# Attention scores of four head pairs in one PE step, steps put off while no bank is idle, and the inverse denominators turned by a transpose

## What is computed

```
h = layer_norm(x); q, k, v = split(h @ w_qkv.T)              # 16 heads of 16 numbers
for each window c of 128 queries and each head:
    scores = q[c] @ concat(k[c-1], k[c]).T * scale             # 128 x 256, masked to a band
    attn = softmax(scores); out[c] = attn @ concat(v[c-1], v[c])
x = x + out @ w_o.T, then norm, a GELU MLP, residual
```

## Time and profile before

| | |
|---|---|
| median of 3 runs | 3789.12 us (3778.06 to 3798.62) |
| profiled execution, its own time | 3792.8 us |
| its span in the trace | 3790.9 us |
| PE busy | 3120.8 us, 82% |
| POOL busy | 2860.8 us, 75% |
| DVE busy | 2831.7 us, 75% |
| ACT busy | 2403.9 us, 63% |
| granted TensorE clock, mean | 0.91 of full speed |

### The profile page before, as it was taken

One profiled execution on the slowest core, in us unless ns is written; L12 is line 12 of the kernel. 1 busy time (PEld: TensorE's weight loads), 2 busy tenths in 40 slices (PEclk: granted clock), 3 DMA queues, 4 the chain that ended last, 5 costly groups with the idle time before them and its releaser, 6 DMA issues.

```text
span 3790.9 us, 58550 instructions
## 1 busy us (share of the span) xinstructions
PE 3120.8 (82%) x17648; PEld 1915.7 (51%) x17648; DVE 2831.7 (75%) x6080; ACT 2403.9 (63%) x5299; POOL 2860.8 (75%) x2511
## 2 busy tenths in 40 slices
PE   5878788887988989798898979889797988977457
PEld 3545354453645546465464636555464654644235
DVE  3357878787787878878787877778788787879860
ACT  5567667575767757676675857667576766754331
POOL 1118889887888879887897978888798878977770
PEclk9998888898999999899898989989998998988678
DMA  2026777777777778776877867787787768789980
GB/s 70 6 78 182 195 193 201 202 206 211 190 209 224 190 216 210 229 196 182 232 212 208 219 200 207 194 225 188 220 213 227 203 185 232 210 241 242 254 224 34
DMA packets 422204, 735.60 MB, mean 194 GB/s; under 512 B 53306, under 2 KB 99010, under 8 KB 421890
## 3 DMA queue, kind: packets, MB, share of 16 engines
q1 hardware_dynamic: 421890, 731.85, 70.7%
HBM read 647.80 MB, written 83.89 MB: 193 GB/s over the span
## 4 chain that ended last, share of the span: by engine, by line
PE 52%; DVE 16%; POOL 10%; ACT 9%; issue 8%; DMA 3%; SPq 1%; DVEq 0%; ACTq 0%; POOLq 0%
PE bank L454 13%; PE bank L462 8%; PE bank L577 6%; PE bank L720 5%; POOL u_rows L1455 5%; PE bank L487 5%; DVE u_rows L1266 4%; POOL u_rows L1448 4%; PE bank L499 4%; PE bank L656 4%; PE bank L708 3%; DMA u_rows<-u_dram 3%; PE bank L515 2%; ACT prob L775 2%; DVE region_b L1198 1%
## 5 line engine op out<-in xcount | busy, mean ns | idle before, releaser
L1455 POOL TENSOR_TENSOR u_rows<-u_rows,c_rows 128x512 f32<-128x512 f32 x1024 | 1339.1, 1311 | 261.9 <-DVE state L1271 208.3
L1448 POOL TENSOR_TENSOR u_rows<-u_rows,b_rows 128x512 f32<-128x512 f32 x960 | 1275.0, 1329 | 33.0 <-DMA u_rows<-u_dram 32.7
L938 ACT ACTIVATE bank<-d_rows,a_rep 128x512 f32<-128x512 f32 x1024 | 697.7, 689 | 283.7 <-DMA d_rows<-delta_dram 127.1
L1266 DVE TENSOR_TENSOR_SCAN u_rows<-bank,state,u_rows 128x512 f32<-128x512 f32 x512 | 642.6, 1270 | 67.6 <-ACT bank L938 64.6
L1266 DVE TENSOR_TENSOR_SCAN u_rows<-bank,u_rows 128x512 f32<-128x512 f32 x512 | 622.7, 1216 | 62.9 <-ACT bank L938 60.4
L656 PE MATMUL bank<-u_rows,sum_n 128*32 128x512 f32 x2048 | 307.1, 674 | 310.3 <-POOL u_rows L1455 303.6
L775 ACT ACTIVATE prob<-prob,neg_max 128x256 f32<-128x256 f32 x1024 | 511.6, 507 | 40.7 <-DVE neg_max L1050 40.4
L1050 DVE CUSTOM_DVE_ANT_0 prob<-bank,band 128x256 f32<-128x256 f32 x896 | 336.9, 416 | 145.5 <-PE bank L487 117.0
L499 PE MATMUL bank<-ident,prob 128*128 128x128 f32 x2048 | 332.4, 290 | 107.2 <-ACT prob L775 66.7
L499 PEld LDWEIGHTS bank<-ident,prob 128*128 128x128 f32 x2048 | 243.1, 147 | 265.0 <-issue 192.1
L487 PE MATMUL bank<-kT,q_own 32*128 32x256 f32 x2048 | 304.3, 417 | 46.4 <-DVE neg_max L1050 26.6
(11 more groups left out here) (163 smaller groups left out, 5661.6 us busy)
## 6 DMA issues: line engine op xcount, KB each, us to landing
u_rows<-u_dram SPq DMA_DIRECT2D x1024, 256.0 KB, 5.5
d_rows<-delta_dram SPq DMA_DIRECT2D x1024, 256.0 KB, 5.3
w<-in_W SPq DMA_DIRECT2D x28, 1024.0 KB
zs_dram<-region_b SPq DMA_DIRECT2D x64, 256.0 KB, 2.2
xc_dram<-region_b SPq DMA_DIRECT2D x64, 256.0 KB, 2.5
delta_dram<-region_b SPq DMA_DIRECT2D x64, 256.0 KB, 2.8
u_dram<-region_b SPq DMA_DIRECT2D x64, 256.0 KB, 2.1
yg<-xc_dram SPq DMA_DIRECT2D x64, 256.0 KB, 5.0
```

The lines of the kernel that those rows point to most:

```text
L938: e.activation(banks[at.bank][:, :], delta_of(i, k), ACT.Exp, scale=a_rep[:, j:j + 1]).then_inc(filled[at.bank], 1)
L1266: e.tensor_tensor_scan(rows, banks[at.bank][:, :], rows, state[:, k:k + 1] if i % 2 else 0.0, ALU.mult, ALU.add).then_inc(drained[at.bank], 1)
L1448: e.tensor_tensor(rows, rows, b_rows[:, :], ALU.mult).then_inc(bx_ready.sem, 1)
L1455: e.tensor_tensor(rows, rows, c_rows[:, :], ALU.mult).then_inc(hc_ready.sem, 1)
```

## The change

1. `scores_of(u)` now does the pairs 4u to 4u+3 at beats 0, 8, 16, ...: four `free` waits at once, then eight matmuls, four for the even heads and four for the odd ones. Four row groups and four banks follow one another.
2. The masks of the four pairs stand at beats 1, 2, 3 and 6 of the eight (before: 1, 2, 5 and 6).
3. `schedule` and `banks_of` become one function that lays out the list and the banks together. At each place it takes the earliest step for which as many banks are idle as it begins uses (and whose thread before it is done); a step for which they aren't is put off.
4. The turn of `rden_wide` is `e.transpose` in the place of `e.matmul` with the identity as the moving operand.

```diff
+MASK_AT = (1, 2, 3, 6)
...
-            out += [(f"s{n}", at, at + 1 + odd), (f"p{n}", at + 5 + odd, at + 6 + 2 * odd)]
+            out += [(f"s{n}", ATT0 + 8 * (n // 4), ATT0 + 8 * (n // 4) + MASK_AT[n % 4]), (f"p{n}", at + 5 + odd, at + 6 + 2 * odd)]
...
+    def earlier(thread, i):
+
+        out = [] if THREADS[thread][0] == ("scan",) else [(thread, i - 1)]
+        if thread:
+            out.append((thread - 1, i | 1 if THREADS[thread][0] == ("fetch",) else i))
+        return out
+
+    order, uses = [], {}
+    idle, counted, signalled = list(range(8)), [0] * 8, [0] * 8
+    while chains:
+        for key, chain in sorted(chains.items(), key=lambda c: c[1][0][:2]):
+            _, _, stage, i, step = chain[0]
+            shared = stage == "scan" and shared_inputs(i, batches)
+            names = begins.get((stage, shared, step), ())
+            if len(names) <= len(idle) and not any(c in chains for c in earlier(*key)):
+                break
+        else:
+            raise AssertionError("no bank is idle")
+        order.append((stage, i, step))
+        for name in names:
             bank = idle.pop(0)
             uses[stage, i, name] = Use(bank, counted[bank], signalled[bank])
...
-            def scores_of(v):
-
-                if v == 0:
+            def scores_of(u):
+
+                if u == 0:
                     for name in ("q0", "q1", "k0", "k1"):
                         e.wait_ge(*gone(use(name)))
-                for n in (2 * v, 2 * v + 1):
+                for n in range(4 * u, 4 * u + 4):
                     e.wait_ge(*free(use(f"s{n}")))
                 for par in range(2):
-                    for n in (2 * v, 2 * v + 1):
+                    for n in range(4 * u, 4 * u + 4):
...
-                e.matmul(banks[at.bank][:, P:2 * P], rden_wide[:, k * P:(k + 1) * P], ident[:, :],
-                         start=True, stop=True).then_inc(filled[at.bank], 1)
+                e.transpose(banks[at.bank][:, P:2 * P], rden_wide[:, k * P:(k + 1) * P],
+                            ident[:, :]).then_inc(filled[at.bank], 1)
...
-                if beat % 4 == 0 and beat < 64:
-                    scores_of(beat // 4)
+                if beat % 8 == 0 and beat < 64:
+                    scores_of(beat // 8)
...
-                v, at = divmod(beat, 4)
-                if at in (1, 2) and v < 16:
-                    masked(2 * v + at - 1)
+                u, at = divmod(beat, 8)
+                if at in MASK_AT and u < 8:
+                    masked(4 * u + MASK_AT.index(at))
```

More of the change, by code:

```diff
@@ L111, in uses_of, with __init__ @@
     return []
+class Use:
+    def __init__(self, bank, n, f):
+        self.bank, self.n, self.f = bank, n, f
 def schedule(batches):
-    at = []
+    chains = {}
     for thread, (stages, lag, begin, end) in enumerate(THREADS):
@@ L119, in schedule @@
         for i in range(2 * batches):
-            spent = 0.0
+            chain, spent = [], 0.0
             for stage in stages:
[L122 to L127, removed]
+                if stage == "route" and i % 2 == 0:
+                    continue
+                which = i // 2 if stage == "route" else i
                 for step, cost in enumerate(COSTS[stage]):
-                    at.append((i + lag + begin + (end - begin) * spent / total, thread, stage, which, step))
+                    chain.append((i + lag + begin + (end - begin) * spent / total, thread, stage, which, step))
                     spent += cost
-    return [(stage, which, step) for _, _, stage, which, step in sorted(at, key=lambda s: s[:2])]
-class Use:
-    def __init__(self, bank, n, f):
-        self.bank, self.n, self.f = bank, n, f
-def banks_of(order, batches):
+            if chain:
+                chains[thread, i] = chain
     begins, ends = {}, {}
@@ L159, in banks_of @@
             idle.append(uses[stage, i, name].bank)
-    return uses
+        del chain[0]
+        if not chain:
+            del chains[key]
+    return order, uses
 def build_block_stack(nc, d):
@@ L185, in build_block_stack @@
     assert WINDOW == P and SEQ % G == 0 and HD == 16 and GROUPS == 2 and ED // EL == TILES and KE * 16 == TILES
-    order = schedule(BATCH)
-    uses = banks_of(order, BATCH)
+    order, uses = schedule(BATCH)
     with ExitStack() as ctx:
```

## The result

| | before | after |
|---|---|---|
| median, 20 runs each | 3791.35 us | 3809.35 us (3800.82 to 3827.49) |
| ratio | | 1.0052, 95% interval 1.0039 to 1.0064 |
| profiled execution, its own time | 3792.8 us | 3806.71 us |
| PE busy | 3120.8 us | 2983.7 us |
| span less PE busy | 670.1 us | 821.2 us |

The forecast was 3759 us and faster; the kernel is slower by 18 us between the medians. The range (3690 to 3865) holds the time, the sign was missed. PE has 137 us less busy time and 151 us more idle time. These two are the whole result, since the span is PE's busy time plus the rest: -137.1 + 151.1 = +14 us in the two profiled executions. By the ratio of the runs the change costs 20 us (0.0052 x 3791).

What follows compares the result with a forecast made beforehand. No engine was taken to bound the whole; PE was busiest, with 52% of the chain. Terms -93 - 11 + 65 + 5 = -34 us from 3792.8 gave 3759 us, range 3690 to 3865 (forecast's own 3725 to 3795, chance 0.32).

Steps and rivals of the forecast that it cites:

- The PE terms: PE's scores with four row groups at once, -93 us, and the turn of rden_wide as a transpose, -11 us.
- The turn's own 11: PE's turn of rden_wide: one record instead of two saves 20 us of PE time, by PE's 52% -11 us.
- Bank hand-overs: PE's refills one step behind a drain: 187 added, 62 waits of 2.0 us, +65 us; bounds 0 and +161.
- ACT's +5: ACT's 65 added refills one step behind a drain delay decays: 22 waits of 1.3 us, by DVE's 16% +5 us.
- The rule read from the earlier trace: Steady period: a shorter PE step can move the end where PE, or PE and POOL, are full, not where DVE is.
- the slow rival: PE's queue in the attention beats: all 187 added bank waits at 1.66 us each, 3855 us; chance 0.26.
- Every close hand-over waits: PE's attention beats: each refill one step behind its drain waits 1.66 us, 310 us idle, 3855 us; chance 0.26.
- Its other sign: PE's granted clock falls below 0.91, beside idle behind drains growing by over 200 us, if every hand-over waits.
- POOL takes the gain: PE's sums wait for POOL, full from 1896 on, so most of the gain goes: -13 us, 3780 us; chance 0.17.
- Don't run together: Scores on PE: the four row groups serialize in pairs, so the first term is 0: 3852 us; chance 0.08.
- Free: Bank hand-overs cost nothing because they fall into PE's idle behind POOL: -104, 3689 us; chance 0.17.
- sign of being wrong: The scores' call on PE over 1.3 us, or PE's added idle outside 60 to 200 us.

Runs made afterwards that it cites:

- e10: The kernel before with each scores matmul issued twice into the same place; 3957.44 us, ratio 1.0451 to the kernel before.
- e9: The change with each scores matmul issued twice; 3863.66 us, ratio 1.0199 to the kernel before.
- e12: The kernel before, transposed-weights uses taking the bank freed last, so refills one step behind their drain go from 48 to 268; 3892.15 us, ratio 1.0274.
- e4: The change with a planner preferring steps whose banks have been idle for two steps or more, moving 962 steps; 3895.98 us, ratio 1.0278 to the kernel before.
- e13: The change with the scan's decays written one beat later (DECAY_AT -1 instead of -2); 3767.18 us, ratio 0.9928 to the kernel before.
- e14: The kernel before with the scan's decays one beat later, as control for e13; 3796.65 us, ratio 1.0024 to the kernel before.
- e18: e13 with weights uses taking the bank freed last, list and work the same; 3895.27 us, ratio 1.0292 to the kernel before.
- e16: The change with four pairs at once for only two of a group's eight fours, and decays one beat later; 3791.32 us, ratio 1.0006 to the kernel before.
- e2: The change with the eight matmuls of a scores call issued two row groups at a time; 3805.86 us, ratio 1.0046 to the kernel before.
- e1: The kernel before with only the turn of rden_wide made a transpose; 3787.74 us, ratio 0.9994 to the kernel before.

## Why the prediction was wrong

**The PE terms held in PE's time; their worth is uncertain.** -93 and -11 were the forecast for 153 us of PE time, -104 together. Busy time fell by 137; the scores' call is 1.15 us in the timeline against 1.13 for a call of half as many before, and the group went to 150.7 (forecast "about 155"). `rden_wide` has one record. The two groups alone fell by 175 us (153.6 and 21.2); the rest of PE's work, unchanged, was busy for longer. At e10's 75% the 137 are worth 103 us, at e9's 54% 74. The forecast's rate was 68% (104 of 153): 70% for the scores, from the 190 us that they had of the chain against 271 us of their calls, and 52% for the turn. That lies between the two. The turn's own 11 was not seen.

**The failed step is "Bank hand-overs".** It took one close refill in three as a wait of 2.0 us, 125 us of idle, and by the chain's 52% +65, with ACT's +5: 70 us. In its place stand 94 to 123 us (the 74 to 103 that PE's time was worth and the measured +20), and by e12's price 88 to 118, inside the bound of 161 that the step had kept. Of the 54 us between -34 and +20, 24 to 53 are this term's and the other 30 to 1 the worth of PE's time; the runs don't settle the split.

The idle time itself came out as forecast, and that was luck. PE's waits on a bank grew by 128 us where 125 stood, but as 118 more waits of 1.1 us, not 62 of 2.0. The rate was taken from one kind of hand-over, the turn behind a convolution. The kind that grew most, scores behind a scan (58.4 us in 53 times), was 4.4 us in 5 times before, and only 28 of the change's close refills are of this kind. A call that wants four banks at once waits for the last of them, close or not: e4 has no close refill at the scores and waits there for 112 us.

What was too small is what the idle costs. 52% of the 128 us is 67; the runs of equal work cost 0.57 to 1 us for each, so 73 to 128. PE's share of the chain says how much of PE's work lies on the path. At a late drain the path runs through the drain instead, as in the chain at 1943 to 1947, and the share of the idle engine says nothing about it; that is read from one place and argued for the others. And e12 showed a cost beside the idle that the step had no term for: PE busy for 32 us longer with the same work.

**The rule read from the earlier trace rows was right and was not used.** "In the first two a shorter PE step can move the end": it can, and by the same reasoning so can a wait put there. DVE at 11.79 of 12 us was named as what makes drains late, but only for the slow rival.

**The rivals.** "Every close hand-over waits" had the right place and direction: PE's queue in the attention beats, drains by DVE and ACT. It put the threshold at 200 us of idle at 52%; PE's waits behind DVE grew from 113 to 215 us and behind ACT from 220 to 284, 165 in all and 128 of them on banks, and that was already enough. Its other sign, a granted clock below 0.91, came with 0.906, but tells little: the kernel before had 0.911 in its profile and 0.908 on average in the runs beside the experiments. "POOL takes the gain" fell: L673's wait behind POOL shrank by 15 where 50 more were asked. "Don't run together" fell, the call is 1.15 us. "Free" fell.

The figure of the Trainium skill ("TensorE: Matmul & The Clock Gate", Part 3, Measured speedup vs the span model: 3.07 for four row tiles) would have made a call 1.33 us, by an estimate from that page's figure, which is for 512 columns. The trace has 1.15 for calls of 256 columns at the full clock, so the measurement stands against it here. The warning cited beside the slow rival (the Trainium skill, "TensorEngine Tiling (Array Packing)", Gotcha 1: PSUM Pressure) points at what decided: a close refill cost 0.29 us by e13 (47 us, and the 9 that e14's later decays cost, over 196), 0.47 by e12 and 0.62 by e18.

**The test of the prediction was too loose.** It asked for 60 to 200 us of new PE idle behind drains, and 128 came, 151 with the other waits. The call of 1.15 us passed as well. Neither sign of being wrong showed, and the forecast was wrong. For all PE time that is saved off the path turns into idle as well (153 less 104 is 49), so a forecast of -34 us already meant about 119 us of idle. A test on span less busy would have had to say 119, and 151 is then plainly too much.

**What stays open.** How much saved PE time is worth: 54% to 75% is from time added, and e16 got 7 us for 39. What a close refill of ACT costs. Why the list of e4 costs 50 us with no more waits on banks. Whether the lower clock alone keeps PE busy for longer where it waits more. A kernel with a fourth `prob` slot was not tried, so theory S is not settled.

## What to carry to other kernels

A step that does more at once also asks for more buffers at once. Count for each buffer how many steps lie between its drain and its refill before and after, and price the added close ones by a run: force close hand-overs in the old kernel with everything else the same. The count is a first guide only; e4 had 28 of them and waited as long as e12 with 268. Where they cost more than the work saved, look for a neighbour that holds a buffer too early; here moving the scan's decays one beat later turned +0.5% into -0.7%. And do not price idle time behind a late drain by the waiting engine's share of the chain: that was 52%, and the runs cost 0.57 to 1.

## What the hardware showed beyond that

**Four row groups run together in full.** Doubling the work of a call tells its slope free of the start. All of these are durations of the timeline at the full clock, where all but a few calls of a run have the same length; a call of the kernel before has 1.13 us (the chain's 1.06 leaves out what overlaps the next). With two row groups (e10 against before) it went from 1.13 us to

```profile
1937.03 2.10 PE L488 MATMUL bank<-kT,q_own 32*128 32x256 f32 x16
```

0.97 us for eight more records. With four (e9 against the change) it went from 1.15 us to

```profile
1907.95 2.12 PE L505 MATMUL bank<-kT,q_own 32*128 32x256 f32 x32 [1.83 <-DVE u_rows L1284]
```

0.97 us for sixteen more. Two more row groups cost nothing there: the means of the calls at the full clock are 1.13 and 2.10 us with two, 1.15 and 2.13 with four. At half the clock, which 6 to 14% of the calls meet in whole or in part, a call is nearly twice as long (2.08 us at most before, 3.97 in e9). Four rounds in 0.97 us are 0.243 each, against 0.216 for one record of 256 columns on the whole array: four products side by side go 3.6 times as fast as one after another (4 x 0.216 over 0.243).

**Issuing the pairs two and two instead of all four in turn** made no difference to a call of eight matmuls (e2): 1.16 us against 1.15.

**A float32 transpose is one record where the product with the identity is two:** 128 records in 43.9 us (343 ns each, in e1, the second line) against 256 in 65.7 in the kernel before.

```profile
L521 PE MATMUL bank<-ident,rden_wide 128*128 128x128 f32 x256 | 65.7, 340 | 0.3 <-POOL rden_wide L1390 0.2
...
L521 PE MATMUL bank<-ident,rden_wide 128*128 128x128 f32 x128 | 43.9, 343 | 0.4 <-POOL rden_wide L1390 0.2
```
